# Last batch of the narrow attention layers: turned scores in alternating PSUM halves, ternary weight and last heads moved up

## Chip, cores and metric

The kernel runs on one core of one Trainium2 chip. The metric is the device time of one execution in microseconds. Times of before: 1531.69 us median of 3 runs (1528.72 to 1532.89).

## What is computed

Eight layers work on x (8 batches of 256 tokens, width 128): four attention layers, each followed by a feed-forward layer. The change touches the two attention layers with 16 narrow heads of 8 columns, called `raw` (layer 0, no weights) and `bias` (layer 4, with projections and biases), and the ternary weights of the feed-forward behind `raw`. In the reference:

```python
def _L0_xattn_ref(Q, K, V):
    ...
    scores = jnp.einsum('bhqd,bhkd->bhqk', q, k) * scale
    scores = jnp.where(causal_mask, scores, jnp.finfo(scores.dtype).min)
    attn = jax.nn.softmax(scores, axis=-1)
    out = jnp.einsum('bhqk,bhkd->bhqd', attn, v)
...
def _ternary(w):
    scale = jnp.maximum(jnp.mean(jnp.abs(w)), 1e-08)
    w_t = jnp.clip(jnp.round(w / scale), -1.0, 1.0)
...
h = jnp.einsum('bsd,fd->bsf', x, _ternary(W1)) + b1
h = jax.nn.gelu(h, approximate=False)
out = jnp.einsum('bsf,df->bsd', h, _ternary(W2)) + b2
...
x = x + _L0_xattn_ref(_layernorm(x, axis=-1), ctx_1024, ctx_1024)
x = x + _L0_ffn_ref(_layernorm(x, axis=-1), L0_ffn_W1, L0_ffn_b1, L0_ffn_W2, L0_ffn_b2)
```

`bias` does the same attention on projected queries, keys and values, and multiplies the heads by an output matrix.

## The kernel before

All engines run programs written out by hand, with semaphores between them. A narrow layer is a software pipeline over the 8 batches, written by `narrow_tensor`, `narrow_scalar`, `narrow_vector` and `narrow_pool`. Its step b runs from -1 to 7. In one step, batch n = b + 1 makes its scores with queries on the partitions (`scores`, in banks 0 to 3) to find each row's maximum (`maxima` on VectorE, L743, half of it from a copy that ScalarE makes in `copy_half`, L616). Batch b makes its scores a second time, turned, with keys on the partitions (`turned_scores`, in banks 4 to 7). The maxima, put into spare columns of the queries, are subtracted by the product itself.

The turned scores of a batch come as three sets of 2048 columns, k = 0, 1, 2. Set 0 (L453, L458) is the second half of the keys against the second half of the queries, sets 1 and 2 (L466, L470) are the first half of the keys for two halves of the heads. ScalarE takes the exponential of each whole set (`exps`, L631) into one of four slots of SBUF. A set waits for the exponential of the one before it, by this line in `turned_scores`:

```python
pe.wait_ge(n_exp, 3 * A.g(b) + k)
```

Between the sets of batch b stand the scores of batch n, but in the last step (b = 7) there is no batch n. Behind the sets come `weighted` (L488, L491: values by exponentials, in banks 0 and 1; half 0 needs exponentials 0 and 1, half 1 needs exponential 2), `heads_out` on ScalarE (L637), `turn_back` on TensorE (L503) and `finish` on VectorE (L750, L755: the division by the sums). In `raw`, GpSimd then adds the heads to x (`add_heads`, L867). In `bias`, TensorE turns the heads (`turn_heads`, L510), ScalarE copies them (`turned_heads`, L642), TensorE multiplies them by the output matrix (`last_products`, `out_product`, L401), and VectorE adds the product to x (`add_out`, L715).

In the last step, VectorE prepares the following feed-forward before it gets to `finish`. In `raw` it makes the ternary weights first (`ternary`: scale L1711 to L1716, then four passes L1719 to L1727 for each of W1T and W2T), from the sum of absolute values that TensorE makes by `abs_total` (L1650, into bank 3). In `bias` it adds the output of batch 6 instead. In both it then takes the statistics of batch 6 (L1555), combines those of 14 tiles (L1561), takes roots, and normalises the 14 tiles (`early_norms`, L1567). TensorE turns 12 of these tiles behind the last batch (`early_turns`, L1590) and ScalarE copies them out. The last two tiles can only be normalised when the last batch has been added to x. TensorE then turns the last group of four tiles, and the dense products of the feed-forward follow (L1675 and on in `ffn0`).

## Time and profile before

| | |
|---|---|
| median of 3 runs | 1531.69 us |
| lowest, highest | 1528.72, 1532.89 us |
| profiled execution, own time | 1534.03 us |
| its span | 1532.1 us |
| busy: TensorE, weight loads, VectorE, ScalarE, GpSimd | 91%, 62%, 66%, 59%, 44% |
| mean granted clock of TensorE | 0.969 |
| chain that ended last | PE 70%, DVE 12%, ACT 8%, issue 7%, POOL 3% |
| last turned set of `raw` starts | 153.32 us |
| last turned set of `bias` starts | 952.14 us |

How to read it: PE is TensorE, PEld its weight loads, DVE is VectorE, ACT is ScalarE, POOL is GpSimd. L453 is line 453 of the kernel. A timeline merges repeated instructions into a row, with the time from the start of the first to the end of the last, and in brackets the idle time before them with what ended it. The chain that ended last is followed back from the last instruction, at each step to what released it. The two narrow layers stand at about 10 to 162 us and 800 to 962 us of the span.

### The profile page before, as it was taken

The page shows a single profiled execution, that of the slowest core. Times are in us where ns is not written, and L with a number is a line of the kernel's source. Part 1 is how long each engine was busy: PE and PEld are TensorE (multiplying, and loading weights), DVE is VectorE, ACT ScalarE, POOL GpSimd, SP SyncE. Part 2 cuts the span into 40 slices and gives each one's busy share as a digit, 9 for nine tenths or more (in the row PEclk, how much of TensorE's full clock was granted, in tenths as well). Part 3 has the DMA queues.
Part 4 walks back from the last instruction along what each step waited for, and adds up shares of the span by engine and source line. Part 5 has one row for each costly group of instructions (what it writes and reads, how often), then busy time and mean ns, then how long its engine had stood idle before and what let it go on. Part 6 is the DMA issues. An engine that isn't in the chain of part 4 may idle for free.

```text
span 1532.1 us, 30474 instructions
## 1 busy us (share of the span) xinstructions
PE 1388.9 (91%) x9625; PEld 952.0 (62%) x9625; DVE 1017.2 (66%) x3557; ACT 905.3 (59%) x1883; POOL 680.2 (44%) x936
## 2 busy tenths in 40 slices
PE   5998989999999778887878888999899999998998
PEld 2454457777777567776754554544467777776665
DVE  5566377776676689989965554443586666666466
ACT  3666456666666478787745665433376666664422
POOL 4442035555554399999954330000064444442300
PEclk9999999999999799899999999899999999999999
DMA  2007000000000000000000000000000000000000
GB/s 67 19 19 280 27 7 5 4 3 3 3 3 1 28 1 1 1 1 0 1 1 1 1 2 1 28 1 0 3 5 5 3 3 3 3 1 1 1 14 14
DMA packets 12667, 21.79 MB, mean 14 GB/s; under 512 B 3088, under 2 KB 9120, under 8 KB 11936
## 3 DMA queue, kind: packets, MB, share of 16 engines
q1 hardware_dynamic: 12576, 20.63, 3.9%
q8 instruction: 50, 0.82, 0.2%
q14 instruction: 41, 0.34, 0.1%
HBM read 19.58 MB, written 1.05 MB: 13 GB/s over the span
## 4 chain that ended last, share of the span: by engine, by line
PE 70%; DVE 12%; ACT 8%; issue 7%; POOL 3%; DVEq 0%; DMA 0%; ACTq 0%; POOLq 0%; SPq 0%
PE bank L981 8%; PE bank L1016 7%; PE bank L994 6%; PE bank L947 4%; PE bank L968 4%; PE bank L2023 4%; PE bank L2269 3%; PE bank L948 3%; DVE sb_both L1990 3%; PE bank L960 3%; PE bank L424 3%; POOL sb_KM L1916 2%; PE bank L466 2%; ACT sb_both L631 2%; PE bank L430 2%
## 5 line engine op out<-in xcount | busy, mean ns | idle before, releaser
L1276 POOL TENSOR_TENSOR sb_both<-sb_both,sb_winv 128x512 f32<-128x512 f32 x256 | 260.9, 1040 | 452.3 <-DVE sb_winv L1195 452.3
L1085 ACT ACTIVATE sb_both<-sb_both,sb_wneg 128x256 f32<-128x256 f32 x512 | 253.0, 495 | 126.3 <-DVE sb_wneg L1189 126.2
L1916 POOL TENSOR_TENSOR sb_KM<-sb_OT 128x1024 f32<-128x1024 f32 x128 | 240.1, 1913 | 19.3 <-ACT sb_OT L1866 9.6
L1189 DVE CUSTOM_DVE_ANT_0 sb_both<-bank,sb_pen 128x256 f32<-128x256 f32 x512 | 182.0, 420 | 0.1
L1804 PE MATMUL bank<-sb_ident,sb_both 128*128 128x128 f32 x1024 | 136.7, 284 | 47.3 <-DVE sb_both L1990 25.2
L1990 DVE SCALAR_TENSOR_TENSOR sb_both<-sb_KM,sb_best,bank 128x1024 f32<-128x1024 f32 x128 | 158.7, 1273 | 14.4 <-ACT bank L1884 13.7
L1884 ACT ACTIVATE bank<-sb_KM 128x1024 f32<-128x1024 f32 x128 | 130.1, 1024 | 49.4 <-DVE sb_both L1990 30.8
L1804 PEld LDWEIGHTS bank<-sb_ident,sb_both 128*128 128x128 f32 x1024 | 117.8, 146 | 61.6 <-DVE sb_both L1990 35.4
L994 PE MATMUL bank<-sb_ident,sb_both 128*128 128x128 f32 x1024 | 134.1, 273 | 8.6 <-DVE sb_QT L1202 5.8
L994 PEld LDWEIGHTS bank<-sb_ident,sb_both 128*128 128x128 f32 x1024 | 118.3, 141 | 27.1 <-issue 12.6
L981 PE MATMUL bank<-sb_KM 64*128 64x256 f32 x1024 | 128.2, 390 | 0.0
L1016 PE MATMUL bank<-sb_QT,sb_VP 128*64 128x256 f32 x1024 | 124.6, 385 | 3.2 <-DVE sb_QT L1202 1.6
L1202 DVE COPY sb_QT<-bank 128x512 f32<-128x512 f32 x128 | 87.9, 687 | 35.7 <-PE bank L994 34.0
L981 PEld LDWEIGHTS bank<-sb_KM 64*128 64x128 f32 x1024 | 93.9, 187 | 19.7 <-issue 8.0
L1016 PEld LDWEIGHTS bank<-sb_QT,sb_VP 128*64 128x64 f32 x1024 | 68.7, 136 | 50.9 <-issue 21.9
L1085 ACT ACTIVATION_READ_ACCUMULATOR sb_both<-sb_both,sb_wneg 128x1 f32 x512 | 95.9, 187 | 0.0
L1095 ACT ACTIVATE sb_QT<-bank 128x512 f32<-128x512 f32 x128 | 75.2, 587 | 28.9 <-PE bank L994 28.9
L743 DVE TENSOR_REDUCE sb_VP<-bank 128x4 f32<-128x1024 f32 (+1 forms) x48 | 58.7, 1224 | 36.0 <-PE bank L430 35.7
L616 ACT ACTIVATE sb_xnT_all<-bank 128x1024 f32<-128x1024 f32 x48 | 49.0, 1022 | 55.8 <-PE bank L430 55.8
L1076 ACT ACTIVATE sb_KM<-bank 128x512 f32<-128x512 f32 x64 | 38.3, 598 | 57.5 <-PE bank L948 57.5
L2331 DVE TENSOR_TENSOR sb_both<-bank,sb_both 128x512 f32<-128x512 f32 x48 | 33.2, 691 | 56.5 <-ACT sb_both L2306 31.2
L1159 DVE COPY sb_KM<-bank 128x512 f32<-128x512 f32 x64 | 44.1, 689 | 40.0 <-PE bank L948 39.9
(293 smaller groups left out, 2720.8 us busy)
## 6 DMA issues: line engine op xcount, KB each, us to landing
sb_ctxT_in<-in_ctxT SPq DMA_DIRECT2D x24, 128.0 KB, 2.3
sb_F<-in_F SPq DMA_DIRECT2D x2, 1024.0 KB
sb_XO<-in_ctx SPq DMA_DIRECT2D x8, 128.0 KB, 2.0
sb_WKQ<-in_WKQ SPq DMA_DIRECT2D x1, 1024.0 KB, 8.9
...
```

The source lines that it names most:

```text
L981: last = pe.matmul(s[:, h, i, :], QK[rows, t, 0, i * P:(i + 1) * P], QK[rows, t, 1, :], start=True, stop=True)
L994: last = pe.transpose(bank[4 + i][:, n * P:(n + 1) * P], PRW[:, t % 4, h, i, kt * P:(kt + 1) * P], ident[:])
L1016: last = pe.matmul(bank[6][rows, (t % 2) * SEQ:(t % 2 + 1) * SEQ], VW[:, kt, (2 * t + h) * 64:(2 * t + h + 1) * 64], PTW[:, t % 2, h, kt, ...
L1085: last = act.activation(p, p, ACT.Exp, scale=-1.0, bias=wneg[:, t % 4, h, i:i + 1], accum_out=wsum[:, t % 4, h, i:i + 1])
L1095: act.activation(PTW[:, t % 2, :, :, P:2 * P], bank[5][:].rearrange("p (h i q) -> p h i q", h=2, i=TPB), ACT.Copy).then_inc(w_pt[1], 1)
L1189: dve.tensor_tensor_reduce(PRW[:, t % 4, h, i, :], s[:, h, i, :], mask, -1.0, BIG, ALU.add, ALU.min, wneg[:, t % 4, h, i:i + 1]).then_inc( ...
L1202: dve.tensor_copy(PTW[:, t % 2, :, :, 0:P], bank[4][:].rearrange("p (h i q) -> p h i q", h=2, i=TPB))\
L1276: pool.tensor_tensor(p, p, winv[:, t % 4, :, i:i + 1].broadcast_to([P, 2, SEQ]), ALU.mult).then_inc(w_norm, 1)
L1804: last = pe.matmul(weight_bank(c), gated[:, h % 4, c * P:(c + 1) * P], ident[:], is_transpose=True, start=(h == 0 and c % 4 == 0), stop=(h ...
L1884: act.activation(sig_bank(h), pairsum[:, h % 4, :], ACT.Sigmoid).then_inc(sig_ready, 1)
L1916: pool.tensor_tensor(dst, s[:, h, 0, :].unsqueeze(2).broadcast_to([P, NK, NK]), s[:, h, 1, :].unsqueeze(1).broadcast_to([P, NK, NK]), ALU. ...
L1990: dve.scalar_tensor_tensor(out=gated[:, h % 4, :], in0=pairsum[:, h % 4, :], scalar=best[:, t % 2, h, TOPK - 1:TOPK], in1=sig_bank(h), op0 ...
```

## The change

Five edits, all for the last step or the one before it:

- `turned_home`: set 1 of the last batch (b = 7, k = 1) goes to banks 0 to 3, not 4 to 7, in both layers, and its exponential reads it there.
- Its waits: set 1 of the last batch waits no longer for an exponential, but for the heads of batch 6 to be copied out of banks 0 and 1, and for the reader of bank 3 (`raw`: the scale) or bank 2 (`bias`: the add of batch 6). Set 2 waits for the exponential of set 0, not of set 1.
- `ternary` is split. The scale and W1T's four passes run one step earlier on VectorE, behind the maxima of batch 7 and ahead of the finish of batch 6. W2T's passes stay.
- `abs_total` runs one step earlier on TensorE, behind the turned scores of batch 6 and ahead of their weighted sums.
- In `bias`, the heads of batch 6 (the seventh) are turned ahead of set 0 of batch 7, and their output product stands between set 0's masks and its own products. On ScalarE their copy goes ahead of the first exponential.

```diff
@@ -353,6 +353,10 @@
 
             return psum[:, first * GROUP:(first + 4) * GROUP].rearrange("p (r n) -> p r n", r=4)
 
+        def turned_home(b, k):
+
+            return 0 if b == BATCH - 1 and k == 1 else 4
+
         def narrow_tensor(pe, A, following):
             WQ, WK, WV, WO = weights.get(A.kind, (None,) * 4)
             biased_kind = A.kind == "bias"
@@ -444,14 +448,20 @@
                     last.then_inc(n_t, 1)
 
             def turned_scores(b, k):
+                at = turned_home(b, k)
                 if k == 0:
                     pe.wait_ge(n_qa, 2 * A.g(b) + 2)
                     pe.wait_ge(n_ka, A.g(b) + 1)
                     if b >= 1:
                         pe.wait_ge(n_fin, 2 * A.g(b - 1) + 2)
+                    ahead = b == BATCH - 1 and biased_kind
+                    if ahead:
+                        turn_heads(b - 1, bank[2])
                     for r in range(4):
                         pe.matmul(bank[4 + r][:], triB[:, 0, :], identB[:].unsqueeze(1).broadcast_to([P, 4, P]),
                                   start=True, stop=False)
+                    if ahead:
+                        last_products(b - 1, bank[2])
                     for half_ in range(2):
                         for r in range(4):
                             rows = slice(32 * r, 32 * r + 32)
@@ -459,14 +469,23 @@
                                              KV[rows, b % 2, half_, P:2 * P],
                                              QA[rows, 2 * half_:2 * half_ + 2, 0:P], start=False, stop=half_ == 1)
                 else:
-                    pe.wait_ge(n_exp, 3 * A.g(b) + k)
+                    if b < BATCH - 1:
+                        pe.wait_ge(n_exp, 3 * A.g(b) + k)
+                    elif k == 2:
+                        pe.wait_ge(n_exp, 3 * A.g(b) + 1)
+                    else:
+                        pe.wait_ge(n_ot, 2 * A.g(b - 1) + 2)
+                        if biased_kind:
+                            pe.wait_ge(n_added, b)
+                        else:
+                            pe.wait_ge(ffn.scale_ready, 1)
                     half_ = k - 1
                     for r in range(4):
                         rows = slice(32 * r, 32 * r + 32)
-                        pe.matmul(bank[4 + r][:], KV[rows, b % 2, half_, 0:P], QA[rows, 2 * half_:2 * half_ + 2, :],
+                        pe.matmul(bank[at + r][:], KV[rows, b % 2, half_, 0:P], QA[rows, 2 * half_:2 * half_ + 2, :],
                                   start=True, stop=False)
                     for r in range(4):
-                        diag = bank[4 + r][:].rearrange("p (s n) -> p s n", s=2)[:, :, P:2 * P]
+                        diag = bank[at + r][:].rearrange("p (s n) -> p s n", s=2)[:, :, P:2 * P]
                         last = pe.matmul(diag, triB[:, 0, :], identB[:].unsqueeze(1).broadcast_to([P, 2, P]),
                                          start=False, stop=True)
                 last.then_inc(n_st, 1)
@@ -533,16 +552,11 @@
                 for k in range(3):
                     if n < BATCH:
                         scores(n, k)
-                    if b == BATCH - 1 and not biased_kind and k == 0:
-                        pe.wait_ge(n_copied, 3 * A.g(b) + 3)
-                        ffn.abs_total(pe)
                     if b >= 0:
                         turned_scores(b, k)
-                    if b == BATCH - 1 and biased_kind:
-                        if k == 0:
-                            turn_heads(b - 1, bank[2])
-                        if k == 1:
-                            last_products(b - 1, bank[2])
+                if n == BATCH - 1 and not biased_kind:
+                    pe.wait_ge(n_copied, 3 * A.g(n) + 3)
+                    ffn.abs_total(pe)
                 if b >= 0:
                     weighted(b, 0)
                     weighted(b, 1)
@@ -628,7 +642,7 @@
                 user = b - 2 if k == 0 else b - 1
                 if user >= 0:
                     act.wait_ge(n_av, 2 * A.g(user) + 2)
-                act.activation(narrow_slot(b, k), score_banks(4), ACT.Exp, scale=8 ** -0.5).then_inc(n_exp, 1)
+                act.activation(narrow_slot(b, k), score_banks(turned_home(b, k)), ACT.Exp, scale=8 ** -0.5).then_inc(n_exp, 1)
 
             def heads_out(b, half_):
                 act.wait_ge(n_av, 2 * A.g(b) + half_ + 1)
@@ -656,10 +670,10 @@
                 for k in range(3):
                     if n < BATCH:
                         copy_half(n, k)
+                    if b == BATCH - 1 and biased_kind and k == 0:
+                        turned_heads(b - 1, bank[2])
                     if b >= 0:
                         exps(b, k)
-                    if b == BATCH - 1 and biased_kind and k == 0:
-                        turned_heads(b - 1, bank[2])
                 if b >= 0:
                     for half_ in range(2):
                         heads_out(b, half_)
@@ -783,11 +797,14 @@
                         context(m)
                 if n < BATCH:
                     maxima(n, 2)
+                if n == BATCH - 1 and not biased_kind:
+                    ffn.ternary_scale(dve)
+                    ffn.ternary(dve, 0)
                 if b == BATCH - 1:
                     if biased_kind:
                         add_out(b - 1, bank[2])
                     else:
-                        ffn.ternary(dve)
+                        ffn.ternary(dve, 1)
                     early(b - 1)
                     ffn.early_moments(dve, following)
                     root(dve, 0, EARLY, following.ln)
@@ -1705,7 +1722,7 @@
 
         groups(act, body)
 
-    def ternary(dve):
+    def ternary_scale(dve):
 
         dve.wait_ge(abs_sum, 1)
         dve.tensor_scalar(half[:], bank[3][:, 0:2], 1.0 / (512 * D), 1e-8, ALU.mult, ALU.max)\
@@ -1715,17 +1732,20 @@
         dve.wait_ge(scale_ready, 2)
         dve.tensor_scalar(half[:], half[:], 0.5, None, ALU.mult).then_inc(scale_ready, 1)
         dve.wait_ge(scale_ready, 3)
-        for n, wt in enumerate((W1T, W2T)):
-            dve.tensor_scalar(below, wt[:], neghalf[:, n:n + 1], None, ALU.is_lt).then_inc(tern_step, 1)
-            dve.wait_ge(tern_step, 4 * n + 1)
-
-            dve.scalar_tensor_tensor(out=above, in0=wt[:], scalar=half[:, n:n + 1], in1=below,
-                                     op0=ALU.is_gt, op1=ALU.subtract).then_inc(tern_step, 1)
-            dve.wait_ge(tern_step, 4 * n + 2)
-            dve.tensor_tensor(below, above, wt[:], ALU.subtract).then_inc(tern_step, 1)
-            dve.wait_ge(tern_step, 4 * n + 3)
-            dve.tensor_tensor(wt[:], wt[:], below, ALU.add).then_inc(tern_step, 1)
-            dve.wait_ge(tern_step, 4 * n + 4)
+
+    def ternary(dve, n):
+
+        wt = (W1T, W2T)[n]
+        dve.tensor_scalar(below, wt[:], neghalf[:, n:n + 1], None, ALU.is_lt).then_inc(tern_step, 1)
+        dve.wait_ge(tern_step, 4 * n + 1)
+
+        dve.scalar_tensor_tensor(out=above, in0=wt[:], scalar=half[:, n:n + 1], in1=below,
+                                 op0=ALU.is_gt, op1=ALU.subtract).then_inc(tern_step, 1)
+        dve.wait_ge(tern_step, 4 * n + 2)
+        dve.tensor_tensor(below, above, wt[:], ALU.subtract).then_inc(tern_step, 1)
+        dve.wait_ge(tern_step, 4 * n + 3)
+        dve.tensor_tensor(wt[:], wt[:], below, ALU.add).then_inc(tern_step, 1)
+        dve.wait_ge(tern_step, 4 * n + 4)
 
     def vector0(dve, A, before_last):
         norm_vector(dve, A)
...
```

TensorE's program at the end of `raw`, from the last set of batch 6 to the last set of batch 7, before (`sb_KM` and `sb_both` hold exponentials):

```order
L470 MATMUL bank<-sb_identB,sb_triB 128x2x128 x4
L488 MATMUL bank<-sb_KM,sb_VP 32x256 x4
L491 MATMUL bank<-sb_KM,sb_VP 32x128 x4
...
L503 MATMUL bank<-sb_ident,sb_OT 128x128 x8
L1650 MATMUL bank<-sb_abssum,sb_onesF 128x2
L453 MATMUL bank<-sb_identB,sb_triB 128x512 x4
L458 MATMUL bank<-sb_OT,sb_QT 128x256 x8
L466 MATMUL bank<-sb_OT,sb_QT 128x512 x4
L470 MATMUL bank<-sb_identB,sb_triB 128x2x128 x4
L466 MATMUL bank<-sb_OT,sb_QT 128x512 x4
L470 MATMUL bank<-sb_identB,sb_triB 128x2x128 x4
```

and now:

```order
L489 MATMUL bank<-sb_identB,sb_triB 128x2x128 x4
L1667 MATMUL bank<-sb_abssum,sb_onesF 128x2
L507 MATMUL bank<-sb_KM,sb_VP 32x256 x4
...
L522 MATMUL bank<-sb_ident,sb_OT 128x128 x8
L461 MATMUL bank<-sb_identB,sb_triB 128x512 x4
L468 MATMUL bank<-sb_OT,sb_QT 128x256 x8
L485 MATMUL bank<-sb_OT,sb_QT 128x512 x4
L489 MATMUL bank<-sb_identB,sb_triB 128x2x128 x4
L485 MATMUL bank<-sb_OT,sb_QT 128x512 x4
L489 MATMUL bank<-sb_identB,sb_triB 128x2x128 x4
```

The product `sb_abssum,sb_onesF` moves from behind the turning back to ahead of the weighted sums. The rest keeps its order; only banks and waits of the second set change.

VectorE's program at the same place, before, from the last maxima of batch 7:

```order
L743 TENSOR_REDUCE sb_VP<-sb_xnT_all 128x2x2x2
L750 RECIPROCAL sb_ninv<-bank 128x16
L755 TENSOR_TENSOR sb_xn_all<-bank,sb_ninv 128x8x8 x2
L750 RECIPROCAL sb_ninv<-bank 128x16
L755 TENSOR_TENSOR sb_xn_all<-bank,sb_ninv 128x8x8 x2
L1555 BN_STATS sb_stats<-sb_x 128x6 x2
L1711 TENSOR_SCALAR sb_half<-bank 128x2
L1714 TENSOR_SCALAR sb_neghalf<-sb_half 128x2
L1716 TENSOR_SCALAR sb_half<-sb_half 128x2
...
L1727 TENSOR_TENSOR sb_W1T<-sb_W1T,sb_gT 128x512
L1719 TENSOR_SCALAR sb_gT<-sb_W2T,sb_neghalf 128x512
```

and now:

```order
L757 TENSOR_REDUCE sb_VP<-sb_xnT_all 128x2x2x2
L1728 TENSOR_SCALAR sb_half<-bank 128x2
L1731 TENSOR_SCALAR sb_neghalf<-sb_half 128x2
L1733 TENSOR_SCALAR sb_half<-sb_half 128x2
L1739 TENSOR_SCALAR sb_gT<-sb_W1T,sb_neghalf 128x512
...
L1747 TENSOR_TENSOR sb_W1T<-sb_W1T,sb_gT 128x512
L764 RECIPROCAL sb_ninv<-bank 128x16
L769 TENSOR_TENSOR sb_xn_all<-bank,sb_ninv 128x8x8 x2
L764 RECIPROCAL sb_ninv<-bank 128x16
L769 TENSOR_TENSOR sb_xn_all<-bank,sb_ninv 128x8x8 x2
L1572 BN_STATS sb_stats<-sb_x 128x6 x2
L1739 TENSOR_SCALAR sb_gT<-sb_W2T,sb_neghalf 128x512
```

Seven instructions, the scale and the four passes over W1T, now stand ahead of the finish of batch 6.

TensorE's program at the end of `bias`, from the turning back of batch 6 (L503 before, L522 now) to the last set of batch 7, before:

```order
L503 MATMUL bank<-sb_ident,sb_OT 128x128 x8
L401 MATMUL bank<-sb_WO,sb_XO 128x128 x2
L453 MATMUL bank<-sb_identB,sb_triB 128x512 x4
L458 MATMUL bank<-sb_OT,sb_QT 128x256 x8
L510 MATMUL bank<-sb_ident,sb_xn_all 128x128 x2
L466 MATMUL bank<-sb_OT,sb_QT 128x512 x4
L470 MATMUL bank<-sb_identB,sb_triB 128x2x128 x4
L401 MATMUL bank<-sb_WO,sb_XO 128x128 x2
L466 MATMUL bank<-sb_OT,sb_QT 128x512 x4
L470 MATMUL bank<-sb_identB,sb_triB 128x2x128 x4
```

and now:

```order
L522 MATMUL bank<-sb_ident,sb_OT 128x128 x8
L405 MATMUL bank<-sb_WO,sb_XO 128x128 x2
L529 MATMUL bank<-sb_ident,sb_xn_all 128x128 x2
L461 MATMUL bank<-sb_identB,sb_triB 128x512 x4
L405 MATMUL bank<-sb_WO,sb_XO 128x128 x2
L468 MATMUL bank<-sb_OT,sb_QT 128x256 x8
L485 MATMUL bank<-sb_OT,sb_QT 128x512 x4
L489 MATMUL bank<-sb_identB,sb_triB 128x2x128 x4
L485 MATMUL bank<-sb_OT,sb_QT 128x512 x4
L489 MATMUL bank<-sb_identB,sb_triB 128x2x128 x4
```

The turning of batch 6's heads and their output product (`sb_WO,sb_XO`) stood behind the first and the second set, and now stand ahead of the first set's products.

## Rows read from the trace of the kernel before

**Rows 1.** Timeline, TensorE, end of the first narrow layer: start us, duration us, instructions [idle before <-releaser].
```profile
140.93 0.64 PE L488 MATMUL bank<-sb_both,sb_VP 128*32 128x256 f32 x8 [0.53 <-ACT sb_both L631]
...
144.17 0.28 PE L1650 MATMUL bank<-sb_abssum,sb_onesF 128*128 128x2 f32 x2
145.28 1.02 PE L453 MATMUL bank<-sb_identB,sb_triB 128*128 128x512 bf16 x4 [0.83 <-DVE sb_xn_all L755]
...
149.38 1.14 PE L466 MATMUL bank<-sb_OT,sb_QT 32*128 32x512 f32 x8 [2.00 <-ACT sb_both L631]
...
153.32 2.09 PE L466 MATMUL bank<-sb_OT,sb_QT 32*128 32x512 f32 x8 [1.97 <-ACT sb_KM L631]
...
158.34 0.64 PE L488 MATMUL bank<-sb_KM,sb_VP 128*32 128x256 f32 x8
...
167.17 0.66 PE L1590 MATMUL bank<-sb_ident,sb_xn_all 128*128 128x128 f32 x4 [0.88 <-DVE sb_xn_all L1567]
```

**Rows 2.** Timeline, ScalarE, same stretch: the exponentials of the last batch.
```profile
147.45 1.88 ACT L631 ACTIVATE sb_both<-bank 128x2048 f32<-128x2048 f32 x1 [3.30 <-PE bank L458]
151.39 1.88 ACT L631 ACTIVATE sb_KM<-bank 128x2048 f32<-128x2048 f32 x1 [2.06 <-PE bank L470]
156.41 1.88 ACT L631 ACTIVATE sb_KM<-bank 128x2048 f32<-128x2048 f32 x1 [3.14 <-PE bank L470]
```

**Rows 3.** Windows, TensorE: stretch, length, busy us (instructions), granted clock, DMA share, GB/s.
```profile
150.00:152.00 2.00, 1.35 (x12) 0.66 1.03 393
156.00:158.00 2.00, 2.00 (x30) 0.63 0.05 14
520.00:540.00 20.00, 13.72 (x42) 0.51 0.00 0
```

**Rows 4.** Timeline, VectorE, end of the first narrow layer.
```profile
138.53 1.21 DVE L743 TENSOR_REDUCE sb_VP<-sb_xnT_all 128x8 f32<-128x1024 f32 x1
143.94 0.26 DVE L750 RECIPROCAL sb_ninv<-bank 128x16 f32<-128x16 f32 x1 [4.19 <-PE bank L503]
...
145.45 0.14 DVE L1711 TENSOR_SCALAR sb_half<-bank 128x2 f32<-128x2 f32 x1
...
148.97 0.49 DVE L1719 TENSOR_SCALAR sb_gT<-sb_W2T,sb_neghalf 128x512 f32<-128x512 f32 x1
...
151.72 0.49 DVE L1555 BATCH_NORM_STATS2 sb_stats<-sb_x 128x6 f32<-128x128 f32 x2
...
156.12 3.68 DVE L1567 TENSOR_SCALAR sb_xn_all<-sb_x,sb_mv,sb_rstd 128x128 f32<-128x128 f32 x14
160.47 0.26 DVE L750 RECIPROCAL sb_ninv<-bank 128x16 f32<-128x16 f32 x1 [0.67 <-PE bank L503]
```

**Rows 5.** Timeline, GpSimd, end of the first narrow layer.
```profile
161.98 0.73 POOL L867 TENSOR_TENSOR sb_x<-sb_x,sb_xn_all 128x256 f32<-128x256 f32 x1 [16.04 <-DVE sb_xn_all L755]
```

**Rows 6.** Timeline, TensorE, end of the second narrow layer.
```profile
950.01 0.61 PE L401 MATMUL bank<-sb_WO,sb_XO 128*128 128x128 f32 x4
952.14 1.14 PE L466 MATMUL bank<-sb_OT,sb_QT 32*128 32x512 f32 x8 [1.52 <-ACT sb_KM L631]
...
958.51 1.47 PE L1590 MATMUL bank<-sb_ident,sb_xn_all 128*128 128x128 f32 x12
960.35 0.44 PE L510 MATMUL bank<-sb_ident,sb_xn_all 128*128 128x128 f32 x2 [0.36 <-DVE sb_xn_all L755]
```

**Rows 7.** Timeline, ScalarE, end of the second narrow layer.
```profile
946.56 1.88 ACT L631 ACTIVATE sb_both<-bank 128x2048 f32<-128x2048 f32 x1 [3.30 <-PE bank L458]
948.34 0.38 ACT L642 ACTIVATE sb_XO<-bank 128x256 f32<-128x256 f32 x1
...
953.87 1.88 ACT L631 ACTIVATE sb_KM<-bank 128x2048 f32<-128x2048 f32 x1 [1.77 <-PE bank L470]
```

**Rows 8.** Timeline, VectorE, end of the second narrow layer.
```profile
950.66 0.42 DVE L715 TENSOR_TENSOR sb_x<-bank,sb_x 128x256 f32<-128x256 f32 x1 [5.56 <-PE bank L401]
...
955.50 3.68 DVE L1567 TENSOR_SCALAR sb_xn_all<-sb_x,sb_mv,sb_rstd 128x128 f32<-128x128 f32 x14
```

1 line of the change is left out of this document (added).

## The prediction

> **What bounds the kernel now.** I read the timeline of each engine at the end of the two narrow layers first, since the change touches nothing else, then the windows for the clock, then asked of each wait what comes next. No other layer's work runs beside these, and the next layer waits for their last batch, so a microsecond gained at the end of one is a microsecond of the whole, if every engine on the way gains it.
>
> In the first layer the last batch makes its three sets of turned scores one after another in banks 4 to 7. The exponential of one must be read out before TensorE may write the next, so the two engines take turns. There, [rows 1] shows TensorE idle 2.00 us and 1.97 us before the second and third set, and [rows 2] the exponentials of 1.88 us each starting at 147.45, 151.39 and 156.41. From the start of a set to its exponential it is 2.01 us for the second (149.38 to 151.39) and 3.09 us for the third (153.32 to 156.41). In the second narrow layer the same step takes 1.73 us (952.14 to 953.87, [rows 6, 7]). The difference, 0.28 + 1.36 = 1.64 us, is TensorE's clock: [rows 3] has it at 0.66 on average from 150 to 152 and at 0.63 from 156 to 158. Of its two levels, 1.00 (2.4 GHz) and 0.50 (1.2 GHz), that makes a fall at 150.64 and a rise at 157.48. Before the fall TensorE had idled 0.83 us (145.28) and 2.00 us (149.38).
>
> Behind the exponentials come the weighted sums, the turning back, and on VectorE the finish of the batch (L750, L755). It waits for TensorE, but for only 0.67 us [rows 4]: VectorE spends 145.45 to 159.80 on the ternary weights and the early norms. So **two chains end within 0.67 us of each other**, and a gain on one alone would be worth 0.67 us. In the second narrow layer VectorE is the later one: its early norms run from 955.50 for 3.68 us to 959.18 [rows 8], while TensorE began turning the early norms back at 958.51, having done the batch's own heads, and waited 0.36 us for the finish at 960.35 [rows 6].
>
> **First layer, part by part.**
> (a) The second set goes to banks 0 to 3. It no longer waits for the first exponential and starts behind the first set, near 147.3; it needs 1.73 us and is done by 149.05. The first exponential ends at 147.45 + 1.88 = 149.33. The second follows at once; a follower starts 1.78 us after such an exponential's start ([rows 7]: 946.56 and 948.34), so at 149.2. The third set waits for the first exponential as before the second did (149.38), is ready at 149.38 + 1.73 = 151.1, and the second exponential ends at 151.1 too. So the third exponential starts at 151.1, not 156.41: **5.3 us earlier**, 1.64 of them the clock. TensorE's idle there shrinks to some 0.4 + 0.1 us, so I take the clock to stay up. The last weighted sums move from 158.34 to 153.0, and TensorE has turned back the batch by 155.7.
> (b) The scale and the first ternary weight leave VectorE's last batch: 145.45 to 148.97, that is **3.52 us** [rows 4]. The second weight (148.97 to 151.72, 2.75 us) stays. The early norms then start at 156.12 - 3.52 = 152.60 and end at 156.28, and the finish, which waits no longer for TensorE (155.7), runs directly behind. In the second layer, where nothing stands between the two, what waits for the finish starts 4.85 us after the norms (955.50 to 960.35, [rows 8, 6]). So GpSimd's add behind it, at 161.98 before [rows 5], starts at 157.45: **4.5 us earlier**. VectorE is now the bound and 0.8 of TensorE's 5.3 us are lost on it.
> (c) What moved up costs nothing: VectorE is free from 139.74 to 143.94 (4.19 us idle, [rows 4]) and the moved part takes 3.52, so 0.67 us of cover remain. If it were late, all of the excess would land on the finish of batch 6 and thus on the last batch. The sum of the absolute values on TensorE (0.28 us, [rows 1]) goes in front of weighted sums that wait 0.53 us for an exponential later on (140.93, [rows 1]), so it is hidden, too. Its input was made in batch 3 and the copy that it waits for (L616) is over before the last maximum starts at 138.53.
> (d) The new waits of the second set (bank 3 read for the scale, heads of batch 6 copied out of bank 1) are met early: the copied heads are turned back by TensorE before its 144.17 in [rows 1].
>
> **Second narrow layer.** (e) The turning of batch 6's heads (0.44 us, as at 960.35) and its output product (0.61 us at 950.01, [rows 6]) move ahead of the first set's own products. By these durations that is 1.05 us; neighbouring groups overlap by 0.15 us each, so I take 0.75. The copy between them (0.38 us on ScalarE, [rows 7]) hides behind the four long masks. The first exponential starts at 946.56 + 0.75 = 947.3 instead. Then as in (a): second set by 948.9, second exponential at 949.1, third set begun at 949.2 and ready at 950.95, third exponential at 950.97 against 953.87: **2.9 us earlier**. The second set also waits for VectorE's add of batch 6 (0.42 us [rows 8] from 946.25, so 946.7), which is met before TensorE arrives at 947.2. TensorE starts turning the early norms at 958.51 - 2.9 = 955.6 and would come to the last batch's heads at 956.95 (1.47 us less an overlap).
> (f) On VectorE that same add moves from 950.66 to about 946.3, and with it the early norms by 4.36 us, to end at 954.8. The finish now waits for TensorE and ends near 956.4. So the last heads are turned at 956.95 instead of 960.35: **3.4 us earlier**, TensorE being the bound by 0.5 us. The 0.5 us by which 3.4 exceeds 2.9 are its old wait of 0.36 us and that overlap.
>
> **The sum** is 4.5 + 3.4 = 7.9 us. The profiled execution took 1534.03 us (span 1532.1), so 1526.1 by it. It lies 2.3 us above the median of the three runs shown and 1.1 above the highest. Against the median the sum gives 1531.69 - 7.9 = **1523.8 us**. A change within 0.3% (4.6 us) can hardly be told from none here, which puts the line at 1527.1.
>
> **Bounds.** In an execution whose clock does not fall in the first layer today, TensorE's chain there is 1.64 us shorter and VectorE's becomes the bound 0.67 us earlier, so the first layer gives 3.85 instead of 4.5. Cost (e) lies between 0.4 (the two hide behind each other) and 1.05 us, so 3.1 to 3.75 for the second layer. The clock is the larger unknown.
>
> **Rivals.**
> 1. *The clock falls in a new place.* Before it turns the last group TensorE waits 0.88 us ([rows 1], 167.17). TensorE's early work now ends 5.3 us earlier, but what it waits for only 4.5, so the gap grows to about 1.8 us, near the 2.00 us after which the clock fell. A fall would stand just ahead of a dense stream. Its price lies between the 1.64 us of above and half of the stretch seen low, from 150.64 to 157.48 or 6.8 us [rows 3], so 3.4. Gain 4.5 to 6.3 us, 1525.4 to 1527.2. Against it: the gap is a little shorter, and no other of that kind stands just before it. Chance 0.25. The Trainium skill (TensorE: Matmul & The Clock Gate, "Part 1: The HAM clock gate") says that the activity monitor runs free of the kernel's start, so that the same kernel falls in different places from run to run; by it this rival would come true in some runs and not in others. The three times of before, 4.2 us apart, would fit that, but no row here shows it.
> 2. *The pair does not run back to back.* If ScalarE reading banks 4 to 7 and TensorE writing 0 to 3 slow each other, or VectorE turns out as the bound in both layers by more than I see, one of the old waits (1.97 and 1.52 us, [rows 1, 6]) stays in each layer, and some overlap with it: gain about 4, 1527.7. Against it: scores into banks 0 to 3 run beside exponentials of banks 4 to 7 all through the layer, and those keep their 1.88 us. Chance 0.10.
> 3. *Slower.* The clock is what could do it, over the rest of the program: [rows 3] has a stretch from 520 to 540 at 0.51. Mean granted clock is 0.969, so some 6.2% of the span, 95 us, is at half rate. All layers behind are shifted by 4.5 to 7.9 us; should that put 25 us more at the low level, 12.5 us would be lost and the kernel be 4.6 us slower (1536.3). It decides from 16 us more on, where the gain is gone. Against it: three executions agree within 4.2 us. Chance 0.03.
> 4. *More than I count*: the clock also stays up somewhere behind where it falls now: gain 10 to 11, 1521. Chance 0.10.
> 5. *It does nothing*, since the next layer waits for something else, a weight load. Then 1531.7. The matmuls behind start within a tenth of the normed values, so hardly. Chance 0.02.
>
> My forecast, gain 6.3 to 9.5, keeps 0.50. The range takes it with rival 4's and most of rival 1's times: 1520.8 to 1527.6. **Faster** by over 0.3% are the forecast, rival 4 and nearly all of rival 1 with some of rival 2: 0.87. Within 0.3%: 0.10. Slower: 0.03.
>
> **What would show it.** Right: in both layers the second and third exponential of the last batch directly behind the first (starts 1.8 us apart), the third near 151.1 and 951 less the first layer's gain; the finish in the first layer without a wait behind the norms, GpSimd's add near 157.5; TensorE idle some 1.8 us before the last group; the first ternary weight done before the finish of batch 6. Wrong: a wait of VectorE for the scale near 140; an exponential above 1.9 us; the second set of the second layer waiting for the add; a clock below 1.00 between 160 and 166, or a mean clock that has moved by more than 0.005.

## Result and profile after

The changed kernel takes **1520.36 us**, median of 6 runs (1518.38 to 1525.95), against 1531.12 (1524.63 to 1532.89) for the kernel before in runs taken beside it. The ratio is 0.9942, with a 95% interval of 0.9922 to 0.9963: 8.9 us less, 5.7 to 11.9. The two medians alone lie 10.8 us apart; I go by the ratio. The forecast was 7.9 us and 1523.8. The same kernel timed again later gave 1519.0 and 0.9924 (0.9900 to 0.9949), or 11.6 us (7.8 to 15.3).

The profiled execution took 1525.95 us, with a span of 1523.8 and a mean granted clock of 0.975, against 1534.03, 1532.1 and 0.969. From the page of the changed kernel, busy times and the chain that ended last:

```profile
PE 1381.9 (91%) x9625; PEld 948.1 (62%) x9625; DVE 1018.4 (67%) x3557; ACT 905.1 (59%) x1883; POOL 680.1 (45%) x936
...
PE 68%; DVE 12%; ACT 8%; issue 7%; POOL 4%; DVEq 0%; DMA 0%; ACTq 0%; POOLq 0%; SPq 0%
```

TensorE is busy for 7.0 us less (1388.9 before), and idle for 1.3 us less. To see where, I cut both spans at the same five instructions and asked for the windows (the stretch up to the first cut, 145.28 us and 145.30, is left out). The cuts are: the first mask product of the last batch in `raw`; the product behind the last group of early norms, with which the dense stream begins; the end of batch 6's finish in `bias`; the first gate product behind `bias`; the turning of the gates. Columns: stretch, length, TensorE's busy us (instructions), granted clock, DMA share, GB/s. Before:

```profile
145.28:168.59 23.31, 16.62 (x138) 0.85 0.47 183
168.59:944.25 775.66, 688.02 (x5125) 0.96 0.01 4
944.25:962.55 18.30, 12.93 (x141) 1.00 0.00 1
962.55:984.51 21.96, 20.23 (x59) 0.69 0.14 49
984.51:1532.10 547.59, 529.70 (x2983) 0.99 0.01 4
```

And after:

```profile
145.30:164.56 19.26, 14.25 (x138) 1.00 0.54 207
164.56:936.34 771.78, 682.03 (x5125) 0.97 0.01 4
936.34:951.21 14.87, 12.38 (x140) 1.00 0.01 2
951.21:972.78 21.57, 18.53 (x59) 0.76 0.14 50
972.78:1523.80 551.02, 533.05 (x2983) 0.98 0.01 4
```

Three of the stretches serve as measures from here on: **R** (end of `raw`, 23.31 to 19.26), **B** (end of `bias`, 18.30 to 14.87) and **G** (gate stage, 21.96 to 21.57). R and B are what the change edits, and they give 4.05 and 3.43 us, 7.48 together. The long stretch between them gave 3.88 more and the last one took 3.43 back, with the same number of instructions and another mean clock (0.96 to 0.97, 0.99 to 0.98). I don't count these two as the change's doing: in the second trace of the same changed kernel they last 774.75 and 547.48 us, close to 775.66 and 547.59 of the kernel before.

End of `raw`, the changed kernel, TensorE's timeline (start, duration, instructions, idle time before and its releaser), against [rows 1]:

```profile
145.30 1.02 PE L461 MATMUL bank<-sb_identB,sb_triB 128*128 128x512 bf16 x4 [1.02 <-DVE sb_xn_all L769]
...
147.22 1.04 PE L485 MATMUL bank<-sb_OT,sb_QT 32*128 32x512 f32 x8
...
149.40 1.14 PE L485 MATMUL bank<-sb_OT,sb_QT 32*128 32x512 f32 x8 [0.59 <-ACT sb_both L645]
...
153.05 0.64 PE L507 MATMUL bank<-sb_KM,sb_VP 128*32 128x256 f32 x8 [0.37 <-ACT sb_KM L645]
...
163.14 0.66 PE L1607 MATMUL bank<-sb_ident,sb_xn_all 128*128 128x128 f32 x4 [1.67 <-DVE sb_xn_all L1584]
164.56 1.13 PE L1692 MATMUL bank<-sb_xnT_all,sb_W1T 128*128 128x512 f32 x2 [0.77 <-ACT sb_xnT_all L1612]
```

ScalarE, against [rows 2]:

```profile
147.47 1.88 ACT L645 ACTIVATE sb_both<-bank 128x2048 f32<-128x2048 f32 x1 [3.37 <-PE bank L468]
149.24 3.75 ACT L645 ACTIVATE sb_KM<-bank 128x2048 f32<-128x2048 f32 x2
```

VectorE, against [rows 4]:

```profile
143.95 0.26 DVE L764 RECIPROCAL sb_ninv<-bank 128x16 f32<-128x16 f32 x1 [1.02 <-PE bank L522]
...
145.46 0.78 DVE L1739 TENSOR_SCALAR sb_gT<-sb_W2T,sb_neghalf 128x512 f32<-128x512 f32 x1
...
152.92 3.68 DVE L1584 TENSOR_SCALAR sb_xn_all<-sb_x,sb_mv,sb_rstd 128x128 f32<-128x128 f32 x14
156.51 0.25 DVE L764 RECIPROCAL sb_ninv<-bank 128x16 f32<-128x16 f32 x1
```

GpSimd, against [rows 5]:

```profile
145.23 0.72 POOL L884 TENSOR_TENSOR sb_x<-sb_x,sb_xn_all 128x256 f32<-128x256 f32 x1 [15.59 <-DVE sb_xn_all L769]
157.79 0.72 POOL L884 TENSOR_TENSOR sb_x<-sb_x,sb_xn_all 128x256 f32<-128x256 f32 x1 [11.83 <-DVE sb_xn_all L769]
```

The three exponentials are one run now: the second and third stand as one row of 3.75 us, which begins 1.77 us behind the first. The waits of 2.00 and 1.97 us on TensorE became none and 0.59. The clock stays at 1.00 through R. VectorE finishes directly behind the early norms, with no wait, where it waited 0.67 us. VectorE is the bound.

End of `bias`, TensorE, against [rows 6]:

```profile
939.22 1.04 PE L485 MATMUL bank<-sb_OT,sb_QT 32*128 32x512 f32 x8
...
941.39 1.14 PE L485 MATMUL bank<-sb_OT,sb_QT 32*128 32x512 f32 x8 [0.59 <-ACT sb_both L645]
...
949.07 0.38 PE L529 MATMUL bank<-sb_ident,sb_xn_all 128*128 128x128 f32 x2
...
951.21 2.85 PE L2116 MATMUL bank<-sb_gateW,sb_xnT_all 128*128 128x8 f32 x24 [0.57 <-DVEq L826]
```

ScalarE, against [rows 7]:

```profile
939.46 1.88 ACT L645 ACTIVATE sb_both<-bank 128x2048 f32<-128x2048 f32 x1 [2.03 <-PE bank L468]
941.24 3.75 ACT L645 ACTIVATE sb_KM<-bank 128x2048 f32<-128x2048 f32 x2
```

VectorE, against [rows 8]:

```profile
938.36 0.43 DVE L729 TENSOR_TENSOR sb_x<-bank,sb_x 128x256 f32<-128x256 f32 x1 [1.16 <-PE bank L405]
...
947.17 0.26 DVE L764 RECIPROCAL sb_ninv<-bank 128x16 f32<-128x16 f32 x1 [0.29 <-PE bank L522]
```

Here TensorE is the bound: the finish waits 0.29 us for it, and TensorE turns the last heads (949.07) without waiting.

### The profile page after: what moved, and what is told of

Same layout as the page of the kernel before. It is cut to its first block, busy times and chain, and to the rows that moved or that the text cites. A ratio compares the mean times of both kernels' runs of the same rounds, so it can differ in the third digit from the quotient of the medians.

```text
span 1523.8 us, 30477 instructions
## 1 busy us (share of the span) xinstructions
PE 1381.9 (91%) x9625; PEld 948.1 (62%) x9625; DVE 1018.4 (67%) x3557; ACT 905.1 (59%) x1883; POOL 680.1 (45%) x936
## 3 DMA queue, kind: packets, MB, share of 16 engines
HBM read 19.58 MB, written 1.05 MB: 14 GB/s over the span
## 4 chain that ended last, share of the span: by engine, by line
PE 68%; DVE 12%; ACT 8%; issue 7%; POOL 4%; DVEq 0%; DMA 0%; ACTq 0%; POOLq 0%; SPq 0%
PE bank L998 8%; PE bank L1033 7%; PE bank L1011 6%; PE bank L964 4%; POOL sb_KM L1936 4%; PE bank L985 4%; PE bank L2043 4%; PE bank L2289 3%; PE bank L965 3%; DVE sb_both L2010 3%; PE bank L977 3%; PE bank L428 3%; PE bank L485 2%; ACT sb_KM L645 2%; PE bank L2382 2%
```

## Experiments

Twelve runs follow, in three groups. The kernel before ran beside each group, with medians of 1531.65 us (31 runs), 1529.56 (19) and 1530.83 (13), and each ratio is to those of its own group. The diffs are against the changed kernel, where nothing else is said, and show the lines that matter.

### Each part alone

**Banks alone in `raw`.** The alternation of halves only there; scale and ternary weight stay in the last step.

```diff
-            return 0 if b == BATCH - 1 and k == 1 else 4
+            return 0 if b == BATCH - 1 and k == 1 and kind in ('raw',) else 4
...
-                    if b < BATCH - 1:
+                    if b < BATCH - 1 or A.kind not in ('raw',):
...
-                if n == BATCH - 1 and not biased_kind:
-                    ffn.ternary_scale(dve)
-                    ffn.ternary(dve, 0)
...
+                        ffn.ternary_scale(dve)
+                        ffn.ternary(dve, 0)
                         ffn.ternary(dve, 1)
```

> First narrow layer: alternating halves, but scale and both ternary weights stay in the last step; second narrow layer as before. Measure R, from the first mask product of the last batch to the first dense product of the feed-forward: 23.31 us before, 19.26 us with the whole change. My theory (two chains end 0.67 us apart, VectorE is the next bound): the three exponentials run back to back, but VectorE's early norms do not move and the finish runs directly behind them, R about 22.4, the kernel about 1 us faster. Rival (the turn taking of TensorE and ScalarE alone is the bound): R about 19.3 or below, the kernel 4 us faster or more.

Measured: 1529.26 us (10 runs), ratio 0.9992 (0.9978 to 1.0006), R 22.70. ScalarE at the end of `raw` in this kernel:

```profile
145.83 1.88 ACT L650 ACTIVATE sb_both<-bank 128x2048 f32<-128x2048 f32 x1 [3.30 <-PE bank L468]
147.60 3.75 ACT L650 ACTIVATE sb_KM<-bank 128x2048 f32<-128x2048 f32 x2
```

The exponentials run back to back as in the changed kernel, the last of them 5.3 us sooner after the start of the batch than before, and R gives 0.61 us of it. VectorE in the same stretch:

```profile
154.51 3.68 DVE L1588 TENSOR_SCALAR sb_xn_all<-sb_x,sb_mv,sb_rstd 128x128 f32<-128x128 f32 x14
158.10 0.24 DVE L769 RECIPROCAL sb_ninv<-bank 128x16 f32<-128x16 f32 x1
```

The finish follows the norms without a wait: the 0.67 us of [rows 4] are gone and VectorE is the bound, as forecast for one half alone. The clock fell here too, but late, at 157.7, between the early turnings, so 0.61 is not the wait's price alone. The start of GpSimd's add settles what the alternation gave: it comes 15.71 us after the batch's first mask product (143.66 to 159.37), against 16.70 before (145.28 to 161.98). In the run of heads ahead alone, further down, `raw` is untouched and its clock did not fall, and there it is 15.71 too (again 143.66 to 159.37). So beside an execution without the fall, the alternation alone gains nothing: VectorE is the bound already.

**Ternary weight alone in `raw`.** The reverse: VectorE's work and `abs_total` moved up, all turned scores in banks 4 to 7.

```diff
-            return 0 if b == BATCH - 1 and k == 1 else 4
+            return 0 if b == BATCH - 1 and k == 1 and kind in () else 4
...
-                    ahead = b == BATCH - 1 and biased_kind
+                    ahead = False
...
-                    if b < BATCH - 1:
+                    if b < BATCH - 1 or A.kind not in ():
```

> First narrow layer: only scale and first ternary weight (and the sum of absolute values) moved up; all turned scores in banks 4 to 7 as before. My theory: VectorE is ready 3.5 us earlier and waits for TensorE instead, R stays 23.3 if the clock falls as before, down to 21.7 if it does not; the kernel within 1.6 us of before. Rival (VectorE's chain is the bound): R about 19.8, the kernel 3.5 us faster.

Measured: 1532.76 us (10 runs), ratio 1.0008 (0.9988 to 1.0028), R 23.59. The finish on VectorE in this kernel:

```profile
161.67 0.26 DVE L769 RECIPROCAL sb_ninv<-bank 128x16 f32<-128x16 f32 x1 [4.03 <-PE bank L522]
```

The wait was 0.67 us and is 4.03: VectorE is 3.4 us sooner, and all of it is spent waiting for TensorE. R grows by 0.28; traces with `raw` untouched differ by as much and more with the place of the clock's fall (23.31, 23.02, and 22.33 where it did not fall).

**Both in `raw`**, `bias` as before.

```diff
-            return 0 if b == BATCH - 1 and k == 1 else 4
+            return 0 if b == BATCH - 1 and k == 1 and kind in ('raw',) else 4
...
-                    ahead = b == BATCH - 1 and biased_kind
+                    ahead = False
...
-                    if b < BATCH - 1:
+                    if b < BATCH - 1 or A.kind not in ('raw',):
```

> First narrow layer as in the change, second as before. My theory: R 19.3; in the second layer B, from the end of batch 6's finish to the first gate product, stays at 18.3 (14.87 with the whole change). The kernel 4.1 us faster, 1527.0, and what goes beyond is the clock elsewhere. Rival (the two layers' gains are not independent, or the clock elsewhere makes up the surplus of the result over 7.9 us): the time lies 2 us or more off that.

Measured: 1525.92 us (10 runs), ratio 0.9975 (0.9957 to 0.9992), or 3.8 us (1.2 to 6.6); R 19.24, B 18.30. Halves that give 0.61 and -0.28 apart give 4.07 together: the two chains are shown. The clock can't stand in for this: its fall in `raw` is worth 0.98 us of R (23.31 against 22.33), and against 22.33 the two halves still give 3.09.

**`bias` alone**, `raw` as before (its ternary weight in the last step, as in the first experiment).

```diff
-            return 0 if b == BATCH - 1 and k == 1 else 4
+            return 0 if b == BATCH - 1 and k == 1 and kind in ('bias',) else 4
...
-                    if b < BATCH - 1:
+                    if b < BATCH - 1 or A.kind not in ('bias',):
...
-                if n == BATCH - 1 and not biased_kind:
-                    ffn.ternary_scale(dve)
-                    ffn.ternary(dve, 0)
...
+                        ffn.ternary_scale(dve)
+                        ffn.ternary(dve, 0)
                         ffn.ternary(dve, 1)
```

> Second narrow layer as in the change, first as before. My theory: B 14.9, R 23.3 (less if the clock happens not to fall), the kernel 3.4 us faster, 1527.7. Rival as for the run before: 2 us or more off that.

Measured: 1525.05 us (10 runs), ratio 0.9965 (0.9949 to 0.9982), or 5.4 us; B 14.86. By the trace the layer gives 3.44, inside that interval (2.8 to 7.8). By the local measures the layers add up: R 19.24 and B 14.86 each alone, 19.26 and 14.87 in the whole change. The totals agree (3.8 and 5.4, or 9.2 us, against 8.9), with intervals too wide to prove it. G is 20.28 here, against 21.96 before.

### Prices and the clock

**Heads ahead alone in `bias`**: turning and output product of batch 6 ahead of the first set, no alternation, `raw` as before. Against the kernel before:

```diff
+                    ahead = b == BATCH - 1 and biased_kind
+                    if ahead:
+                        turn_heads(b - 1, bank[2])
                     for r in range(4):
...
+                    if ahead:
+                        last_products(b - 1, bank[2])
...
-                    if b == BATCH - 1 and biased_kind:
-                        if k == 0:
-                            turn_heads(b - 1, bank[2])
-                        if k == 1:
-                            last_products(b - 1, bank[2])
...
-                    if b >= 0:
-                        exps(b, k)
                     if b == BATCH - 1 and biased_kind and k == 0:
                         turned_heads(b - 1, bank[2])
+                    if b >= 0:
+                        exps(b, k)
```

> Second narrow layer: only the heads of batch 6 and their product moved ahead, all turned scores in banks 4 to 7; first layer as before. My theory (the move costs TensorE 0.75 us on the path and its gain on VectorE is not needed while TensorE and ScalarE take turns): first exponential 0.75 us later after the finish of batch 6 than before (2.31 us), the others 3.65 us apart, B between 18.3 and 18.8. Rival (VectorE's early norms were the bound of this layer): B about 16.

Measured (one execution): 1528.66 us, B 19.89, above the expected 18.3 to 18.8. ScalarE at the end of `bias`, this kernel, where batch 6's finish ended at 937.78:

```profile
940.90 1.88 ACT L645 ACTIVATE sb_both<-bank 128x2048 f32<-128x2048 f32 x1 [2.03 <-PE bank L468]
945.92 1.88 ACT L645 ACTIVATE sb_KM<-bank 128x2048 f32<-128x2048 f32 x1 [3.15 <-PE bank L489]
949.57 1.88 ACT L645 ACTIVATE sb_KM<-bank 128x2048 f32<-128x2048 f32 x1 [1.77 <-PE bank L489]
```

The first exponential starts 3.12 us after that finish, against 2.31 before (944.25 to 946.56): the moved part costs **0.81 us**, and the forecast took 0.75. The second exponential starts 5.02 us after the first, the third 3.65 after the second. 3.65 is the interval at full clock (half of 946.56 to 953.87 in [rows 7]). The 5.02 holds a **fall of the clock in `bias`**, worth 1.37 us on TensorE, where the trace of before has none. With it B can't tell what the moved part costs at the end; the expected B stays untested in an execution without the fall. Its rival, B about 16, is far off. The run of banks alone in `raw` shows a fall there too: exponentials at 939.66, 943.71 and 948.73, 4.05 and 5.02 us apart, and B 19.50 with `bias` untouched. At the end of `raw` it is the other way round. This run's three exponentials there start 3.65 us apart, with no fall, and R is 22.33 with `raw` untouched.

**Waits of `raw` filled.** The kernel before, with eight products that nobody reads (idle products from here on) ahead of each of sets 1 and 2 of the last batch.

```diff
+                    if b == BATCH - 1 and not biased_kind:
+                        for _ in range(8):
+                            pe.matmul(bank[2][:], triB[:, 0, :], identB[:].unsqueeze(1).broadcast_to([P, 4, P]), start=True, stop=True)
```

> Kernel before, but TensorE fills its two waits for exponentials in the last batch of the first layer with 8 idle products each (bf16, 128x512, into bank 2, which nobody reads). My theory: the idle is what brings the clock down there, so with the gaps filled it stays at 1.00 and the exponentials start 3.65 to 3.9 us apart; but VectorE is the next bound, so R falls from 23.31 by 0.7 only, to 22.6. Rival 1 (the clock falls whatever TensorE does there): gaps of 3.9 and 5.0 us as before. Rival 2 (VectorE does not bound): R 21.7.

Measured (one execution): 1535.15 us, R 22.31. TensorE at the end of `raw`, this kernel:

```profile
145.51 1.90 PE L474 MATMUL bank<-sb_identB,sb_triB 128*128 128x512 bf16 x8
...
164.37 0.66 PE L1614 MATMUL bank<-sb_ident,sb_xn_all 128*128 128x128 f32 x4 [1.50 <-DVE sb_xn_all L1591]
165.79 2.07 PE L1699 MATMUL bank<-sb_xnT_all,sb_W1T 128*128 128x512 f32 x2 [0.77 <-ACT sb_xnT_all L1619]
```

With the waits filled the exponentials start 3.65 us apart and R is 1.00 us shorter than in the kernel before. That does not show that the filling kept the clock up. The run before this one has the same two waits unfilled, exponentials 3.65 us apart and R 22.33. Of the four traces with these waits unfilled the clock fell in three (before, ternary weight alone, `bias` alone), and one filled trace without a fall does not separate the two readings. So the idle waits as the cause of the fall in `raw` are plausible and not shown. What is shown is the price of the filling: sixteen idle products in two waits cost R nothing (22.31 against 22.33). The clock fell later instead, at 165, behind waits of 1.50 and 0.77 us: the product at 165.79 takes 2.07 us where the changed kernel has 1.13. That is rival 1's place, but the wait is no longer than the 1.51 us in the run before, where no fall followed. The whole took no less: the mean clock of this execution was 0.968.

**W2T's passes spread**: the changed kernel with the first pass over W2T an iteration earlier and the last behind the finish.

```diff
                     ffn.ternary(dve, 0)
+                    ffn.ternary(dve, 1, (0,))
...
-                        ffn.ternary(dve, 1)
+                        ffn.ternary(dve, 1, (1, 2))
...
                     finish(b, 1)
+                    if b == BATCH - 1 and not biased_kind:
+                        ffn.ternary(dve, 1, (3,))
```

> The changed kernel, with the second ternary weight's four passes spread as well: the first one step earlier behind the first weight, the last behind the finish of the last batch where VectorE waits 0.94 us for GpSimd; two remain in the last step. My theory: VectorE's early norms start 1.3 us earlier and TensorE's turning back (155.9) is the bound again, GpSimd's last add about 1.1 us earlier, R 18.2 instead of 19.26, the kernel 1.1 us faster than the change. Rival (the finish already waited for TensorE, or the pass moved up delays batch 6): R 19.2 or more.

Measured: 1523.37 us (10 runs), ratio 0.9965 (0.9943 to 0.9988), R 18.23: another 1.03 us out of R. The total shows no gain over the changed kernel (ratio 0.9942), so the expected 1.1 us is seen in R alone. In its trace the clock fell at 165, rival 1's place again, behind waits of 1.11 and 0.77 us. VectorE, then GpSimd, in this kernel:

```profile
146.56 1.05 DVE L1748 SCALAR_TENSOR_TENSOR sb_gT<-sb_W2T,sb_half,sb_gT 128x512 f32<-128x512 f32 x1
...
157.63 0.68 DVE L1753 TENSOR_TENSOR sb_W2T<-sb_W2T,sb_gT 128x512 f32<-128x512 f32 x1
```

```profile
146.34 0.73 POOL L887 TENSOR_TENSOR sb_x<-sb_x,sb_xn_all 128x256 f32<-128x256 f32 x1 [15.52 <-DVE sb_xn_all L769]
157.79 1.10 POOL L887 TENSOR_TENSOR sb_x<-sb_x,sb_xn_all 128x256 f32<-128x256 f32 x1 [10.73 <-DVE sb_xn_all L769]
```

I come back to these below: whichever of the two engines starts second takes longer than it does alone.

**Gate stage filled**: the changed kernel with idle products between the groups of gate products behind `bias` (two behind each of the first three, three ahead of the last). A gate product has 8 columns.

```diff
+            if g == GROUPS - 1 and A.index in (2,):
+                idle_products(pe, 3)
             pe.wait_ge(xnT_ready, GROUPS * A.index + g + 1)
...
+            if g < GROUPS - 1 and A.index in (2,):
+                idle_products(pe, 2)
```

> The changed kernel, with idle products (bf16, 128x512, bank 7) in the feed-forward behind the second layer: 2 behind each of the first three groups of gate products and 3 ahead of the last group, where TensorE waits 1.30 and 0.77 us anyway. Let G be the time from the first gate product to the turning of the gates: 21.96 us before, 21.57 after, 20.28 in the run of the second layer alone. My theory (small gate products and waits bring the clock down there for 10 to 14 us): the low stretch shrinks or goes, G 18 to 20.5, the kernel 1 to 3 us faster than the change. Rival (products that fill waits cost what they take, or the clock falls anyway): G 21.5 or more.

Measured: 1519.32 us (10 runs), ratio 0.9934 (0.9908 to 0.9959), G 18.14 against 21.57. By windows of 1 us the clock was low there for 3.4 us, against 10.2. The total (0.9934) can't be told from the changed kernel's (0.9942).

### The change again, and a version that adds up

**The change again**, unedited, beside the three below.

> The changed kernel once more, beside the others on one chip. My theory: R 19.25 and B 14.86 again, all three exponentials back to back in both layers, the kernel 8 to 10 us faster than before (7.9 of the sum and the falls of the clock that it avoids in the second layer, where 3 of 6 runs with the old order show one of 1.4 us). Rival (part of the first result was scatter): 6 us or less.

Measured: 1519.0 us (6 runs, 1514.15 to 1523.19), ratio 0.9924 (0.9900 to 0.9949); R 19.26, B 14.86, G 20.28.

**Heads between the early turnings**: in `bias`, the last batch's heads are turned ahead of the third group of early norms instead of behind it.

```diff
-                turn_heads(BATCH - 1, bank[3])
+                for g in range(GROUPS - 1):
+                    if g == GROUPS - 2:
+                        turn_heads(BATCH - 1, bank[3])
+                    ffn.turn_group(pe, following, g)
```

> The changed kernel, with the turning of the last batch's heads in the second layer placed between the second and third group of early turns, since VectorE's finish ends some 0.5 us before TensorE comes to it. My theory: B 14.4 instead of 14.87; the kernel 0.4 us faster than the change, not told apart from it by time. Rival (the gate products wait for something else, or the third group's copy is late): B 14.8 or more.

Measured: 1522.56 us (8 runs), ratio 0.9935 (0.9909 to 0.9960), B 14.51: 0.35 us locally, nothing that the total could show.

**All of it**: W2T spread, heads between, gate stage filled.

> Change, W2T's passes spread, heads between, and the idle products in the feed-forward behind the second layer. My theory: the three gains are in different places and add up: R 18.2, B 14.4, G 18.1; 1.05 + 0.4 + 1.5 to 3.4 us under the change, so 3 to 5 us faster than it. Rival (what is gained in one place is lost to a fall of the clock in the next): 1 us or less.

Measured: 1518.72 us (6 runs, 1513.15 to 1520.42), ratio 0.9920 (0.9898 to 0.9942); R 18.22, B 14.52, G 17.24. Locally the three gains add up: R, B and G together are 49.98 us against 54.40 in the change again, 4.4 us less. The total misses the expected 3 to 5 us, and the rival, 1 us or less, describes it: 1518.72 against 1519.0. Between the two traces the 4.4 us are lost in three places that the edits don't touch: before the last batch of `raw` (1.28 us, the first rise of the clock, see the last section), between R and B (1.04), and in the gate stage of the last feed-forward layer (1.67, next run).

**All, with more waits filled**: also four and three idle products around the last norms of the feed-forward behind `raw`, two behind the last output product of `bias`, and in the other feed-forward layer with gates one behind each of the first three groups and three ahead of the last.

```diff
+        idle_products(pe, 4, bank[4])
         norm_tensor(pe, A)
+        idle_products(pe, 3, bank[4])
...
+                ffn.idle_products(pe, 2)
```

> As the run before, with idle products also in the waits before the first feed-forward's last group (4 and 3), behind the output product of the last batch of the second layer (2), and in the last feed-forward's gates (1 behind each group, 3 before the last). My theory: the clock falls in none of these places in most runs, R 18.2, G 18 or less, another 1 to 2 us faster. Rival (idle products that outlast the wait they fill cost their own time): R 18.5 or more and no gain over the run before.

Measured: **1512.77 us** (6 runs, 1507.31 to 1516.82), ratio 0.9876 (0.9851 to 0.9901), 19.0 us below the kernel before. TensorE at the gate stage, this kernel (the row of `sb_identB,sb_onesB` is a pair of idle products):

```profile
948.86 1.06 PE L2134 MATMUL bank<-sb_gateW,sb_xnT_all 128*128 128x8 f32 x8
949.77 0.59 PE L2124 MATMUL bank<-sb_identB,sb_onesB 128*128 128x512 bf16 x2
...
954.43 1.06 PE L2134 MATMUL bank<-sb_gateW,sb_xnT_all 128*128 128x8 f32 x8
955.34 7.97 PE L2054 MATMUL bank<-sb_xnT_all,sb_F 128*128 128x512 f32 x18
```

The clock stays at 1.00 in the whole stage, and G is 17.24. This version beats the changed kernel, which in the same group had no run below 1514.15. Its ratio's interval meets that of the change at the edge only. Against the version without the added fills R, B and G are equal (18.23, 14.51, 17.24), and 6 us lie between the medians. Most of what the two traces differ by stands in a stage that R, B and G leave out: the gates of the last feed-forward layer, which this version fills too. From the first gate product there to the first product with `sb_picks`, in the version of all edits and in this one:

```profile
1396.51:1412.67 16.16, 14.70 (x54) 0.79 0.00 1
1394.97:1407.78 12.81, 12.48 (x60) 1.00 0.00 1
```

That is 3.35 of the 4.9 us between the two spans; another 1.38 us are from before the last batch of `raw`. In the thirteen other traces, where this stage is not filled, its clock is 0.69 to 0.88 and it takes 14.48 to 17.00 us, so the filling is worth 1.7 to 4.2 us by these. The fills in `raw` and `bias` show no gain: R and B are as without them. With six runs each I leave open how much of the 6 us will repeat.

## Why the prediction held, and where it was off

**The time** fell inside the range, 3.4 us below the forecast, on the side of rival 4. Against the kernel beside it the gain was 8.9 us where 7.9 was forecast.

**(a)** The second set started at 147.22 (forecast 147.3), the second exponential at 149.24 (149.2). The third is not a row of its own; if it starts half-way through the 3.75 us, that is 151.1, as forecast. The last weighted sums started at 153.05 (153.0). The clock stayed up.

**(b)** The early norms started at 152.92 (152.60), and GpSimd's add at 157.79 (157.45), 4.19 us earlier rather than 4.5. Nearly all that is missing, 0.29 us, is one instruction: the first pass over W2T takes 0.78 us where it took 0.49 [rows 4]. So it does in all six traces where it follows the finish and the statistics of batch 6 directly, and it takes 0.49 in all five with the scale and W1T still ahead of it. It now starts at 145.46, beside GpSimd's add of 145.23 to 145.95. Moving seven instructions away from in front of it put it there. The forecast had costed what it moved, and took for granted that what stayed would keep its durations. The Trainium skill (SBUF — State Buffer, "Who interferes with whom") says that where the two engines contend, whichever issues first has the port pair that VectorE and GpSimd share for the whole instruction, and the other is blocked. The trace agrees in order: VectorE's pass, begun second, outlasts the add by 0.29 us; in the spread version another pass takes 1.05 us in place of 0.75 and outlasts it by 0.54; and there GpSimd's second add, begun 0.16 us after a pass of VectorE, takes 1.10 where it took 0.72. That the block is complete is not shown: each time the second ends behind the first by less than its own duration alone (0.29 of 0.49, 0.54 of 0.75, 0.58 of 0.72 us). From the add to the dense stream 0.16 us more were lost, so 4.03 us arrived, and R, measured from the batch's start, gives 4.05.

**(c)** Nothing waited for the moved part: VectorE is idle for 1.02 us (143.95) in place of 4.19. Cover of 0.67 was forecast. **(d)** No new wait shows ahead of the second set (147.22). TensorE waits 1.02 us ahead of the batch (145.30) in place of 0.83, since `abs_total` no longer fills a part of that wait, and the batch starts where it did.

**(e)** Cost 0.81, forecast 0.75. The third exponential, if it starts half-way through its 3.75 us, at 943.12, comes 6.78 us behind batch 6's finish in place of 9.62: 2.84 us earlier, forecast 2.9. **(f)** B gives 3.43 (3.4), TensorE the bound by 0.29 us (0.5).

**The sum**, 7.9, measured 7.48 in the profiled pair. Its bound for an execution without the fall in `raw` was too mild: in such an execution R is 22.33, so the layer gives 3.07 us there (22.33 to 19.26) and not 3.85. The forecast let all but 0.67 of the clock's 1.64 us hide behind VectorE, and 0.98 came through: from the finish's start to GpSimd's add it took 1.51 us before (160.47 to 161.98, [rows 4, 5]) and 1.27 in such an execution (158.10 to 159.37 in the run of heads ahead alone), so a part of the finish had been waiting for TensorE too, and the wait ahead of it was not all.

**The term that was too small** is the second layer's gain, taken as 3.4 us at the end of the layer and nothing behind it. B gave 3.43 in the profiled pair, as forecast, but the gate stage behind it got shorter too. With the old order the clock falls early in G (mean 0.69, G 21.96 or 21.97 in three traces), or it falls in `bias` first and then in G (B 19.50, 19.89, 19.86 with G 21.21, 20.78, 20.60; the second of these carries (e) as well). B and G together come out nearly the same in all six: 40.26, 40.27, 40.27, 40.71, 40.67 and 40.46 us. A fall in `bias` is thus mostly paid back in the gate stage. With the new order the clock stayed up in `bias` in all eight traces (B 14.51 to 14.87). In the four of them with no further edit in these two stretches it was 0.75 to 0.83 in G, and B and G together were 36.44, 35.14, 34.93 and 35.14. So the second layer's edit is worth 3.8 to 5.8 us down to the turning of the gates, not 3.4. This is rival 4, which had 0.10: the clock stays up for longer somewhere behind, too. The runs show its mechanism. That it is why the medians came out below the forecast they don't show, for 7.9 us lies inside the interval of both comparisons (at the very edge of the second), and the clock moves the time by as much without the change.

**Rival 1** named the right place, but its cause is not shown. TensorE's wait before the last group grew to 1.67 us (forecast 1.8), and in the five traces where it lasted 1.66 or 1.67 us the clock did not fall there. It fell in one of the eight traces that had both parts of the `raw` edit (W2T spread, behind a wait of 1.11) and in the one with the waits of `raw` filled (1.50), but in neither of the changed kernel. The section of the Trainium skill that the prediction cites (TensorE: Matmul & The Clock Gate, "Part 1: The HAM clock gate") tells of the first rise of one kernel coming at different points from run to run; that falls do so as well is what the runs here show. With `raw` untouched the fall came at 150.64 before, at 144.6 in the run of `bias` alone, and not at all in the run of heads ahead alone. The first rise differs too: the changed kernel started `raw`'s last batch at 145.30 in one trace and at 140.57 in the other (the last section shows why). **Rival 2** is refuted: ScalarE kept 1.88 us (3.75 for two) beside TensorE's writes to the other half. **Rival 3 and 5** did not come. The mark that I had set for a wrong forecast, a mean clock moved by more than 0.005, was met (0.969 to 0.975) by a gain; but the move lay within the scatter, 0.968 to 0.980 over all traces here, so the mark was set too tight.
